# A recurrent convolution with a top-k expert layer: a load waited for later, per-tile work in other steps, wider gate products

## The reference, cut to what matters

```python
# layer 1: a recurrence over the 32 rows s, with a convolution along w (3 taps) on the state h
pre = conv(h, w_stos) + b_stos + conv(layernorm_over_channels(x), w_itos masked)[row s]
i, g, f, o = split(pre, 4)
c_new = sigmoid(f) * c + sigmoid(i) * tanh(g)
h_new = c * sigmoid(o)                      # the old c
x = x + all h_new
# layer 2: tokens are the 32 x 32 positions, 64 channels each, normalised over the channels
logits = t_norm @ gate_w.T + gate_b         # 32 experts
probs = softmax over the 1024 tokens; each expert takes its 8 best tokens
pooled = weighted sum of these tokens -> gelu MLP of the expert -> added back to the tokens
x = x + that
```

## Time and profile before

| | |
|---|---|
| median of 3 runs | 266.56 us |
| lowest and highest | 263.29 and 267.12 us |
| the profiled execution | 262.74 us |
| its span (first to last instruction in the trace) | 261.0 us |
| mean granted PE clock | 0.898 |

### The profile page before, as it was taken

The page is one execution under the profiler, slowest core; times in us unless marked ns, Lnnn a source line. Parts: engine busy times, 40 slices in busy tenths (PEclk is TensorE's granted clock), DMA queues, the critical chain, the costliest instruction groups (busy, mean ns, idle before and its releaser), DMA issues.

```text
span 261.0 us, 10681 instructions
## 1 busy us (share of the span) xinstructions
PE 188.6 (72%) x4619; PEld 156.0 (60%) x4619; DVE 169.2 (65%) x632; ACT 107.0 (41%) x249; POOL 126.2 (48%) x111
## 2 busy tenths in 40 slices
PE   0635029898799799799799797629995217788990
PEld 0524017787688698698698696527884215656440
DVE  0497004659869869769769774552784799816881
ACT  2231004545655636636636644431742447361000
POOL 3443002654757967967967975644149710300000
PEclk9975556999999999999999999976999655999998
DMA  6963960030030140130040149983010100000486
GB/s 152 160 115 86 205 114 3 3 82 7 5 84 5 45 84 6 44 87 3 23 109 3 45 127 219 188 175 78 5 44 4 40 1 3 3 3 3 128 283 232
DMA packets 24651, 19.60 MB, mean 75 GB/s; under 512 B 3869, under 2 KB 22557, under 8 KB 24605
## 3 DMA queue, kind: packets, MB, share of 16 engines
q1 hardware_dynamic: 24605, 18.93, 31.8%
HBM read 14.61 MB, written 4.31 MB: 73 GB/s over the span
## 4 chain that ended last, share of the span: by engine, by line
POOL 30%; PE 24%; issue 23%; DMA 9%; DVE 7%; ACT 2%; SPq 1%; POOLq 1%; DVEq 0%; ACTq 0%
PE ps L879 10%; POOL r L371 8%; DMA xc<-in_x 7%; POOL rb_xr L356 6%; POOL r L376 5%; PE ps L1111 5%; PE ps L870 4%; POOL xc L349 4%; POOL xtok L382 4%; POOL x_split L362 3%; DVE st L600 2%; PE ps L1068 1%; DMA scratch<-r1t 1%; POOLq L58 1%; PE ps L935 1%
## 5 line engine op out<-in xcount | busy, mean ns | idle before, releaser
L349 POOL TENSOR_TENSOR xc<-xc,h 128x256 f32<-128x256 f32 x32 | 23.3, 727 | 72.8 <-DVE h_lo L627 72.8
L879 PE MATMUL ps<-x_split,w_hi 64*64 64x256 f16 x1000 | 52.0, 280 | 8.0 <-DVE cell L648 6.5
L879 PE MATMUL ps<-h_hi,w_hi 64*64 64x256 f16 x750 | 33.2, 278 | 13.6 <-DMA xc<-in_x 13.6
L459 ACT ACTIVATE ps<-ps,bias 128x256 f32<-128x256 f32 x32 | 14.3, 448 | 59.1 <-PE ps L879 59.1
L879 PEld LDWEIGHTS ps<-x_split,w_hi 64*64 64x64 f16 x1000 | 26.6, 109 | 16.2 <-DVE cell L648 9.8
L879 PE MATMUL ps<-h_lo,w_hi 64*64 64x256 f16 x750 | 33.4, 278 | 1.6 <-issue 1.6
L879 PE MATMUL ps<-h_hi,w_lo 64*64 64x256 f16 x750 | 33.2, 278 | 0.0
L635 DVE TENSOR_TENSOR h<-cell,ps 128x256 f32<-128x256 f32 x32 | 13.3, 415 | 30.4 <-ACT ps L459 30.2
L879 PEld LDWEIGHTS ps<-h_hi,w_hi 64*64 64x64 f16 x750 | 21.9, 110 | 14.2 <-DMA xc<-in_x 14.0
L879 PE MATMUL ps<-x_split,w_lo 64*64 64x256 f16 x500 | 25.9, 278 | 4.4 <-issue 4.4
L371 POOL TENSOR_TENSOR r<-v,pow_exp 128x16 f32<-128x16 f32 x8 | 23.3, 2913 | 10.6 <-DVE v L594 10.6
(11 more groups left out here) (112 smaller groups left out, 334.3 us busy)
## 6 DMA issues: line engine op xcount, KB each, us to landing
out<-tail_room SPq DMA_DIRECT2D x16, 256.0 KB, 4.0
rb_xr<-scratch SPq DMA_DIRECT2D x14, 256.0 KB, 4.4
w1s<-in_L_ffn_weight SPq DMA_DIRECT2D x1, 2080.0 KB
xc<-in_x SPq DMA_DIRECT2D x2, 1024.0 KB, 11.2
rbf<-scratch SPq DMA_DIRECT2D x28, 64.0 KB, 2.2
xc<-in_x SPq DMA_DIRECT2D x4, 256.0 KB, 4.2
xc<-in_x SPq DMA_DIRECT2D x2, 512.0 KB, 6.4
w_rows<-in_L_conv_w_itos SPq DMA_DIRECT2D x2, 96.0 KB, 3.6
```

Of the source, the lines that this page charges most:

```text
L349: p.tensor_tensor(here, here, h32[:, i % 2, :].rearrange("p (b w) -> p b w", w=W), ALU.add) \
L459: a.activation(pre[O][:, 0:COLS], pre[O][:, 0:COLS], ACT.Sigmoid, bias=bias[:, 3:4]).then_inc(s_sg_o, 1)
L879: ins = pe.matmul(pre[gate][to, 0:COLS], w[half(h), tap, C * GATE_ORDER[gate]:][:, 0:C], data[half(h)], start=first and m == 0, stop=s_don ...
```

## The change

Every instruction stays but the logits products; what changes is where they stand.

1. **The wait for the last load of x.** It leaves the head of the loop and stands in `between(1, 2)` on PE, in front of `turn_in` of tile 4, which is the first to read that load.
2. **Other steps.** On PE the turn of r0 goes from i = 2 to i = 1, the logits from i = 3 to i = 1, and the turn of r1 from i = 1 of the tile after to i = 3 (tile t - 1 instead of t - 2). On POOL `rsqrt0` stands behind the first `scale_rows` and not the second, `rsqrt1` before `residual(t, 3)` and not behind it, and both `scale_tokens` of tile t - 1 end the tile. On DVE the statistics are spread over other steps, `stats0` of the second half is cut into two parts, and the logits are scaled after i = 1. ACT and SP follow. The expert weights now come behind `spread_r1(4)` and no longer before it.
3. **Wider logits products.** Eight products of 128 columns a tile become two of 512.

```diff
@@ SP
             for t in range(NT):
-                if t > 1:
-                    spread_r1(t - 2)
                 if t + 2 < NT:
                     spread_r0(t + 2)
+                if t > 0:
+                    spread_r1(t - 1)
                 if t == NT - 3:
...
-            spread_r1(NT - 2)
@@ POOL
                 residual(t, 0)
                 if t + 1 < NT:
                     scale_rows(t + 1, 0)
+                if t + 2 < NT:
+                    rsqrt0(t + 2)
                 residual(t, 1)
                 if t + 1 < NT:
                     scale_rows(t + 1, 1)
-                if t + 2 < NT:
-                    rsqrt0(t + 2)
                 residual(t, 2)
                 if t + 1 < NT:
                     lo_of_x(t + 1, 0)
-                if t > 1:
-                    scale_tokens(t - 2, 0)
-                if t == NT - 1:
-                    scale_tokens(t - 2, 1)
+                if t > 0:
                     rsqrt1(t - 1)
                 residual(t, 3)
                 if t + 1 < NT:
                     lo_of_x(t + 1, 1)
-                if 1 < t < NT - 1:
-                    scale_tokens(t - 2, 1)
-                if 0 < t < NT - 1:
-                    rsqrt1(t - 1)
-            for k in range(2):
-                scale_tokens(NT - 2, k)
+                if t > 0:
+                    scale_tokens(t - 1, 0)
+                    scale_tokens(t - 1, 1)
@@ DVE, between(t, i) and after(t, i)
-                if i == 0 and 0 < t and u - 1 < NT:
-                    stats0(u - 1, ps_t, 1)
+                if i == 0 and 0 < t and u - 1 < NT:
+                    variances0(u - 1)
...
+                if i == 3 and u < NT:
+                    stats0(u, ps_t, 1, 0, 4)
...
+                if i == 0 and t > 0:
+                    stats1(t - 1, 0, 8)
+                if i == 1 and t > 1:
+                    scale_logits(t - 2)
+                if i == 2 and u < NT:
+                    stats0(u, ps_t, 0)
                 if i == 3 and u < NT:
-                    stats0(u, ps_t, 0)
-                if i == 3 and 1 < t and not last:
-                    scale_logits(t - 2)
+                    stats0(u, ps_t, 1, 4, 8)
@@ PE, logits
-                for g in range(NG):
-                    for j in range(2):
-                        ins = pe.matmul(ps_lg[C * j:C * j + C, TOK * g:TOK * g + TOK], gw[:, :],
-                                        xc[:, 2 * g + j, u, :], start=g == 0, stop=g == NG - 1)
+                for j in range(2):
+                    ins = pe.matmul(ps_lg[C * j:C * j + C, :], gw[:, :], xc[:, j::2, u, :], start=True, stop=True)
@@ PE, between(t, i)
-                if i == 1 and t > 1:
-                    if t + 1 < NT:
-                        pe.wait_ge(s_r0_kept, t + 1)
-                    else:
-                        pe.wait_ge(s_r1_kept, t - 2)
-                    turn_r1(t - 2)
-                if i == 2 and t + 2 < NT:
+                if i == 1 and t + 2 < NT:
...
                     turn_r0(t + 2)
+                if i == 1 and t > 1:
+                    logits(t - 2)
                 if i == 2 and t + AHEAD < NT:
                     wait(pe, s_xtok, 2 * t)
                     pe.wait_ge(s_x_stats, 2 * (t + AHEAD))
+                    if t + AHEAD == X_LOADS[3][0]:
+                        pe.wait_ge(s_x[3], 2 * DMA)
                     turn_in(ps_t, lambda b: xc[:, b, t + AHEAD, :])
...
-                if i == (2 if t == NT - 1 else 3) and t > 1:
-                    logits(t - 2)
+                if i == 3 and t > 0:
...
+                    turn_r1(t - 1)
@@ PE, ahead of the loop
             rows_of_x(0, (O, I))
-            pe.wait_ge(s_x[3], 2 * DMA)
             for n in range(LAST):
```

More of the change, by code:

```diff
@@ L524, in _ @@
                 step(RT * t + 1)
-                if t > 1:
-                    keep_r1t(t - 2)
+                if t + 2 < NT:
+                    keep_r0t(t + 2)
                 if t + 1 < NT:
@@ L529, in _ @@
                 step(RT * t + 2)
-                if t + 2 < NT:
-                    keep_r0t(t + 2)
                 if t + 1 < NT:
@@ L534, in _ @@
                 step(RT * t + 3)
+                if t > 0:
+                    keep_r1t(t - 1)
             keep_logits(NT - 2)
-            keep_r1t(NT - 2)
             a.wait_ge(s_x1_stats, NT + 1)
@@ L595, in variances, with stats0 @@
                     .then_inc(s_var, 1)
-            def stats0(u, banks, k):
+            def stats0(u, banks, k, a=0, z=8):
                 v.wait_ge(s_x_turned, 2 * u + k + 1)
-                for b in range(8):
+                for b in range(a, z):
                     ins = v.bn_stats(st0[:, u % 2, 8 * k + b, :], banks[k][:, C * b:C * b + C])
-                ins.then_inc(s_x_stats, 1)
+                if z == 8:
+                    ins.then_inc(s_x_stats, 1)
             def variances0(u):
@@ L726, in between @@
             def between(t, i):
-                u, last = t + AHEAD, t == NT - 1
+                u = t + AHEAD
                 if i == 0 and 0 < t and u - 1 < NT:
-                    stats0(u - 1, ps_t, 1)
+                    variances0(u - 1)
                 if i == 1 and t > 0:
-                    stats1(t - 1, 0, 8 if last else 4)
-                if i == 2 and 0 < t and not last:
                     stats1(t - 1, 8, 12)
-                if i == 2 and last:
+                if i == 2 and t > 0:
                     variances1(t - 1, t)
-                if i == 3 and 0 < t and not last:
-                    variances1(t - 1, t)
-                if i == 3 and last:
-                    scale_logits(t - 2)
+                if i == 3 and u < NT:
+                    stats0(u, ps_t, 1, 0, 4)
             def after(t, i):
-                u, last = t + AHEAD, t == NT - 1
+                u = t + AHEAD
                 if i == 0 and t == 0:
@@ L747, in after @@
                     keep_gate()
-                if i == 0 and 0 < t and u - 1 < NT:
-                    variances0(u - 1)
+                if i == 0 and t > 0:
+                    stats1(t - 1, 0, 8)
                 if i == 1 and t > 0:
-                    stats1(t - 1, *((8, 16) if last else (4, 8)))
-                if i == 2 and 0 < t and not last:
                     stats1(t - 1, 12, 16)
+                if i == 1 and t > 1:
+                    scale_logits(t - 2)
+                if i == 2 and u < NT:
+                    stats0(u, ps_t, 0)
                 if i == 3 and u < NT:
-                    stats0(u, ps_t, 0)
-                if i == 3 and 1 < t and not last:
-                    scale_logits(t - 2)
+                    stats0(u, ps_t, 1, 4, 8)
             for t in range(NT):
@@ L968, in between @@
                     pe.wait_ge(s_gate_kept, 2)
-                if i == (2 if t == NT - 1 else 3) and t > 1:
-                    logits(t - 2)
+                if i == 3 and t > 0:
+                    if t + 2 < NT:
+                        pe.wait_ge(s_r0_kept, t + 2)
+                    else:
+                        pe.wait_ge(s_r1_kept, t - 1)
+                    turn_r1(t - 1)
             pe.wait_ge(s_const, 2)
@@ L1017, in _ @@
             logits(NT - 2)
-            pe.wait_ge(s_r1_kept, NT - 2)
-            turn_r1(NT - 2)
+            between(NT - 1, RT - 1)
             turn_x1(NT - 1)
```

## The result

| | before | after |
|---|---|---|
| median, lowest and highest of 4 executions, us | 266.84 (263.29 to 267.81) | 245.2 (243.72 to 248.2) |
| ratio of the mean times, 95% interval | | 0.921 (0.909 to 0.934) |
| the profiled execution, us | 262.74 | 248.2 |
| its span, us | 261.0 | 246.4 |
| mean granted PE clock | 0.898 | 0.938 |

The change makes the kernel 8% faster. That rival's mechanism, however, is not what the trace shows.

What follows compares the result with a forecast made beforehand. The prediction took PE's wait for the last load of x as the key bound. Its terms, -13.56 + 4.5 + 0 - 1.0 - 0.9 - 0.75 + 1.3 + 0.6 - 1.5 = -11.3, gave 251.4 profiled, 253.6 with 2.2 added; range 246 to 261.

Steps and rivals of the forecast that it cites:

- I add 2.2: Last step of the sum: 2.2 us added to the profiled execution's 251.4 to forecast the median, 253.6.
- The wait for the load: what goes. 13.56.: Head of the loop: PE's idle time before 37.70, waiting for the last load of x, goes: -13.56 us.
- What is late next: PE's own instructions: First tile: PE's next instruction block, needed at about 29.0, comes at 33.5 under the load of x: +4.5 us.
- The clock: First tile: PE's time at the lower clock after the stall evens out against before: 0.
- r0 hidden beside the stall: First tile: PE's 1.0 us wait for POOL's power of r0 falls beside PE's instruction stall: -1.0 us.
- Tile 1 and tiles 2 to 4: Loop steps: tile 1 saves 0.9 us, tiles 2 to 4 0.25 each, 0.75, with wide logits costing +0.3 a tile.
- Tile 5: Tile 5: no turn of x any more, so PE comes sooner to r1 and waits 1.25: +1.3 us.
- Tile 6, the stalls, tile 7 and tail: Loop's end: tile 6 +0.6, the weights' 7.6 us of stalls stay, tile 7 and tail -1.5 us.
- No stall: Rival, first tile: the instruction block passes the load of x, so PE does not stall; 246.6 us, chance 0.2.
- Whole load: Rival, first tile: the instruction block waits for the whole load of x, stall 10 us; 259.1 us, chance 0.2.
- The POOL rival: Rival, every tile: POOL becomes the bound and its powers delay PE, up to 4.3 us a tile; 280 us, chance 0.04.
- Another transfer in its place: Rival, no change: another transfer waits where the load of x did; 264 us, chance 0.04.

## Why the prediction was right and wrong

The forecast said 251.4 for the profiled execution and added 2.2 for the median. Profiled, after took 248.2: the sum is 3.2 too high. Its median is 3.0 below the profiled execution, where I took +2.2: another 5.2. This second part is the larger. The step that failed is "I add 2.2": an offset between one execution and the median of before was carried to after, where it has the other sign. Why executions of one kernel differ isn't shown, as only one of each kernel was profiled; the mean clock doesn't order them (of before, 263.9 us at 0.889 and 267.02 at 0.928). Before ranges from 261.7 to 267.8 over all its executions, after from 243.7 to 248.2; an execution of either may lie 3 us to one side.

The terms of the sum, on the profiled executions:

- **"The wait for the load: what goes. 13.56."** Right. The first h comes 14.01 sooner. That is 0.45 more, though this execution is some 0.5 us later from the start on (SP issues the first spread at 22.79 and not 22.32): the 31 products behind the load ran at 0.50 and took 2.15 us, and run at 1.00 now.
- **"What is late next: PE's own instructions", 4.5.** The mechanism is right and was seen: blocks of 128 products, 9.1 us from asking to running under the load. The step that failed is the one that picked the block: "asks for the third, and would need it 128 products later, about 29.0. [...] I take 33.5". That one came ahead of the load's large packets. The next was late, and how much that costs depends on what else holds PE in it: 0.83 in after, 2.85 in the kernel with the moved wait alone, 0.5 to 3.1 in the others. So a stall of 0.5 to 3, not 3 to 6.5. This and the wait for POOL below make the first tile and what stands ahead of it 1.7 us better than the sum.
- **"The clock", 0.** Right in size, 6.9 us at 0.51 against 5.9 at 0.50 before, but not by the reason given. The clock was down before the stall of 0.83 began. It stayed up in the first tile behind stalls of 1.89, 2.19, 2.73, 2.85 and 3.06 in other kernels, and fell there behind waits for POOL's power of 1.85 and 2.05, though not behind one of 1.94; and in the kernel with x in two loads it fell right behind a stall of 1.10. What decides it is open.
- **"r0 hidden beside the stall", -1.0.** Wrong in the first tile. The wait came first, 2.05 long, and the stall behind it; and POOL was 1.27 late, since its factors took 5.2 us to land, the later half of them more, and not the 4.0 of the earlier trace rows. Start and tile 0 together: -11.74 against -10.1.
- **Tile 1 and tiles 2 to 4**, -0.9 and -0.75: -1.05 and -0.28. The logits' +0.3 was wrong; they cost what they had cost. The lower bound was the right one, the two halves run beside each other throughout. What took its place is r0's wait, 1.36 and not 0.85. PE arrives at h + 5.60, as forecast (91.68 for an h at 86.08), but POOL ends at h + 6.8, not 6.3. It starts the residual at h + 2.0 and not at 1.4, because DVE makes `h_lo` 1.5 us after h:

```profile
86.08 0.42 DVE L628 TENSOR_TENSOR h<-cell,ps 128x256 f32<-128x256 f32 x1 [0.34 <-ACT ps L452]
86.42 0.81 DVE L579 TENSOR_TENSOR v<-st 128x16 f32<-128x16 f32 x1
...
87.57 0.42 DVE L620 TENSOR_TENSOR h_lo<-h,h_hi 128x256 f16<-128x256 f32 x1
```

  `variances0` stands between h and its low half at i = 0, on the chain to POOL's residual and so to the power. Before, statistics stood there (h_lo 1.39 behind h), but r0's power had a step more. The order of the kernel after shows this; I had read it for the steps and not for this chain.
- **Tile 5**, +1.3: +1.46, right in size. The reason given holds only in part: the wait for r1 is 0.85 there and not 1.25. With 0.78 for the cell and 1.34 for r0 PE waits 2.97 in that tile, where before it waited 0.44 and 0.97.
- **Tile 6, the stalls, tile 7 and tail**, together +0.6 - 1.5: measured -2.9, the 2.0 us that are the other part of the 3.2. "The 7.6 us of stalls stay" failed: they are 5.9, and 0.5 + 4.2 or 2.7 + 4.3 in kernels whose blocks fall otherwise. In kernels without them the steps of tile 7 are 0.6 shorter (12.53 against 13.12), and POOL's chain behind the last h is 1.2 shorter, so that -1.5 for these two was about right.

**The rivals.** "No stall" (246.6) is nearest in time, but wrong as a mechanism, as the stall is there, short. "Whole load" would have needed a restart 1.5 us after the second transfer of x, which landed at 39.69; it was at 37.91. (x was not the deepest load, as the forecast said there: `w1s` is one transfer of 2080 KB.) The POOL rival is refuted: the second power's wait is 0.68 and the tile 19.4; its smaller form, one wait of 1.36, is real and worth 5.5 us when taken away. The forecast named as a sign of being wrong that PE waits at the start for anything but instructions: it did, 2.05 for POOL's power. "Another transfer in its place" was there in small: the spread of the first factors, 1.27 on POOL.

**What the range left out.** All its cases priced the steps' edits at a microsecond or two. The kernel with these alone gained 9.1 by the medians, 4.4 between the profiled executions. In a comparison without the weights' stalls these edits give 0.3 in the loop (172.87 against 172.57). The other 4.5 by which the profiled executions of these two kernels differ are in the tail, where the clock stood lower for longer. How much of this is the order of POOL's last work and how much where the clock happens to fall is not settled: all twelve kernels have one profile each, and their tails range from 63 to 73 us.

## What to carry to other kernels

- When a wait for a large load is taken away, the load itself stays, and PE's instructions share its path. Count PE's products from the start in blocks (128 with their weight loads here), mark the boundaries, and look at which are asked for while the load runs. Under a load it was 6 to 9 us here from asking to running, once 11.7, and what PE runs or waits for meanwhile comes off that. Issuing a load behind the loop bought 6.9 us here, and x in halves around the first spread 3.2. One half a tile later bought nothing.
- In an in-order engine the place of a turn that needs another engine's power matters as much as the place of the power. With the power early, PE waited 1.36 us a tile when it asked for it one step earlier too, and nothing when it asked where it had before.
- One profiled execution per kernel and a median are two measures. When executions of one kernel differ by 4 to 6 us, as here, give the forecast for the median no offset from a single trace.

## What the runs showed of the hardware that was not expected

- 192 instructions fewer on PE made one kernel 9.7 us faster (247.98 to 238.32) although they cost nothing in the tiles where they stand (19.38 and 19.36 us): they move the block boundaries. In another kernel the same edit made no difference that could be told (246.64 and 245.2).
- The instruction block asked for at 28.75, some 2 us into the load of x, came only in the load's last 4 us: none from 26.5 to 34, one at 35.04. The first of the two transfers of x had landed at 34.95. In the six other kernels with the whole load in this place and a product stream beside it the packet also came 0.2 to 1.0 us after that landing, in the one that loads a half there 0.3 ahead of it. The Trainium skill, "DMA: Bandwidth & Descriptors", section Queues, rings and completion order, has an engine turn between queues at packet boundaries, and counts 9 to 17 descriptors to a packet, at most 64. The 1.49 MB in 810 of the profile's packets over 7.5 us, on 16 engines, are 0.15 us each (16 x 7.5 / 810). If each is one descriptor, a turn is some 1.3 to 2.5 us by the page's usual count (an estimate) and 9.5 by its highest; the 6.3 us seen lie between. No run here shows how many of them go in one turn, so the runs leave the cause open.
- Two f32 products of 512 columns on the two halves of the array, issued one after the other, take 1.01 us together (93.24 to 94.25), shown as four entries of 0.62 us in the mean: 2.5 us if they ran in turn. Eight of 128 columns in alternation take 1.02.
- PE's clock fell in after at 35.1, while PE was working, 0.9 us behind a wait of 2.05 for another engine. In the kernel with the moved wait alone it stayed at 1.00 behind a stall of 2.85.
